# Routed experts of an AdaLN + MoE kernel: rows turned two slots ahead, down product one slot later, three expert homes

## The reference, cut to what matters

```python
# 2048 tokens of width 512 (x: 32 x 64 x 512)
x = x + ffn0(cond0(x))          # layer 0: a 64x64 matrix per batch row, then a dense FFN with LoRA experts
x = x + moe1(cond1(x))          # layer 1:
  # scores = softmax(x @ gate_w); top 2 of 8 experts; H = 352, D = 512
  # g      = silu(x @ w_gate[e]) * (x @ w_up[e])
  # routed = sum over the token's two experts of comb[e] * (g @ w_down[e])
  # shared = silu(x @ sw_gate) * (x @ sw_up) @ sw_down          # hidden width 704
```

## Time and profile before

| | |
|---|---|
| median of 3 runs | 1052.67 us (1052.26 to 1055.33) |
| the profiled execution's own time | 1050.97 us |
| its span, first to last instruction | 1049.1 us |
| busy: PE / PEld / VectorE / ScalarE / GpSimd | 96% / 80% / 50% / 30% / 34% of the span |
| the chain that ended last | PE 85%, DMA 4%, POOL 4%, DVE 2%, issue 1%, ACT 1% |
| mean granted TensorE clock | 0.991 |

### The profile page before, as it was taken

The page is one execution under the profiler, slowest core; times in us unless marked ns, Lnnn a source line. Parts: engine busy times, 40 slices in busy tenths (PEclk is TensorE's granted clock), DMA queues, the critical chain, the costliest instruction groups (busy, mean ns, idle before and its releaser), DMA issues.

```text
span 1049.1 us, 14852 instructions
## 1 busy us (share of the span) xinstructions
PE 1011.8 (96%) x4893; PEld 838.6 (80%) x4895; DVE 525.9 (50%) x886; ACT 314.8 (30%) x550; POOL 354.2 (34%) x351
## 2 busy tenths in 40 slices
PE   7999999999999999999999999999989999999993
PEld 5778887888888888788867777778788999999992
DVE  3797877455574545645666433574543314443100
ACT  2743332111122121211242110301034554545451
POOL 4132344510000000000033000022168989899873
PEclk9999999999999999999999999999999999999997
DMA  6478643534343434444335101004155665565433
GB/s 210 159 252 280 191 132 118 175 130 150 117 131 127 146 127 158 160 155 149 116 145 185 41 1 41 1 1 160 66 178 146 163 161 134 141 144 130 80 60 41
DMA packets 51322, 136.41 MB, mean 130 GB/s; under 512 B 8708, under 2 KB 10004, under 8 KB 50772
## 3 DMA queue, kind: packets, MB, share of 16 engines
q1 hardware_dynamic: 37268, 109.22, 30.4%
q0 software_dynamic: 12432, 25.71, 12.3%
q10 hardware_dynamic: 1584, 1.02, 0.3%
HBM read 96.85 MB, written 39.07 MB: 130 GB/s over the span
## 4 chain that ended last, share of the span: by engine, by line
PE 85%; DMA 4%; POOL 4%; DVE 2%; issue 1%; ACT 1%; SPq 1%; PEldq 0%; POOLq 0%; PEld 0%; DVEq 0%; ACTq 0%
PE ps_y L1677 6%; PE ps_y L1679 6%; PE ps_y L1678 6%; PE ps_h L1637 6%; PE ps_h L1636 6%; PE ps_h L1635 5%; PE ps_u L1690 3%; PE ps_u L1689 3%; DMA out_x<-yt,slot_tok 3%; PE ps_h L1923 2%; PE ps_y L1846 2%; PE ps_y L1847 2%; PE ps_h L1830 2%; PE ps_y L1923 2%; PE ps_y L1918 2%; PE ps_h L1831 2%
## 5 line engine op out<-in xcount | busy, mean ns | idle before, releaser
L1194 DVE TENSOR_TENSOR h<-h,wb 128x512 f32<-128x512 f32 x64 | 44.4, 694 | 162.6 <-ACT h L900 161.2
L894 ACT ACTIVATE h<-ps_h,bias 128x512 f32<-128x512 f32 x64 | 44.0, 689 | 235.1 <-PE ps_h L1644 235.1
L685 POOL DMA_DIRECT2D s_raw<-in_sgu x8 | 4.3, 544 | 299.9 <-DVE g_lo L1202 192.1
L1677 PE MATMUL ps_y<-w_hi,g_hi 128*128 (+1 forms) x256 | 102.6, 401 | 2.3 <-DVE g_lo L1202 2.3
L1679 PE MATMUL ps_y<-w_hi,g_lo 128*128 (+1 forms) x256 | 101.6, 397 | 0.0
L1678 PE MATMUL ps_y<-w_lo,g_hi 128*128 (+1 forms) x256 | 101.5, 396 | 0.0
L1635 PE MATMUL ps_h<-xt_hi,w_hl 128*128 128x512 f32 x256 | 100.1, 391 | 0.7 <-ACT lg_t L843 0.7
L1637 PE MATMUL ps_h<-xt_hi,w_hl 128*128 128x512 f32 x256 | 100.4, 392 | 0.0
L1636 PE MATMUL ps_h<-xt_lo,w_hl 128*128 128x512 f32 x256 | 100.2, 391 | 0.0
L1469 DVE CAST eg_hi<-e_raw 128x704 fp32r<-128x704 f32 x32 | 16.7, 581 | 135.4 <-PE ps_y L1948 122.7
L900 ACT ACTIVATE h<-ps_h,bias 128x512 f32<-128x512 f32 x64 | 43.9, 688 | 114.3 <-PE ps_h L1657 114.3
(11 more groups left out here) (319 smaller groups left out, 2459.8 us busy)
## 6 DMA issues: line engine op xcount, KB each, us to landing
w_hl<-w1s_d SPq DMA_DIRECT2D x49, 704.0 KB, 4.1
w1s_d<-w_hl SPq DMA_DIRECT2D x16, 704.0 KB, 5.9
e_raw<-in_wgu SPq DMA_DIRECT2D x8, 1408.0 KB, 7.2
w_raw<-in_w1b SPq DMA_DIRECT2D x16, 608.0 KB, 4.7
x_in<-in_x SPq DMA_DIRECT2D x4, 1024.0 KB, 5.9
xres<-in_x SPq DMA_DIRECT2D x16, 256.0 KB, 4.6
acc<-x_d SPq DMA_DIRECT2D x4, 1024.0 KB, 7.3
xc_d<-xc SPq DMA_DIRECT2D x4, 1024.0 KB, 4.8
```

Of the source, the lines that this page charges most:

```text
L1194: tt(h1[u][:], h1[u][:], wb[:, v, :], ALU.mult).then_inc(gch, 1)
L1677: mm(ps_y[:, j, :], g_hi[u][:, cols], sl(w2_hi), start=first, **kw)
```

## The change

- TensorE's slot becomes gate(t+1), up(t+1), turn_x(t+3), turn_g(t), down(t-1). GpSimd's becomes products(t+1), x_low(t+3), g_low(t), gather(t+5), scatter_add(t-1). ScalarE's becomes silu(t+1), up(t+1), x_high(t+3), g_high(t), weigh(t-1).
- `xg_hi`, `xg_lo`, `rgt_hi` and `rgt_lo` get two buffers each; `xg` has two instead of four.
- Split weights have three homes, numbers 0, 2, 3 of one tensor `expert`; expert e waits for the last down product of expert e-3. A second table, `home_tab`, packs the homes of six slots, `etab` packs six expert numbers; TensorE reads both at each loop head. VectorE computes `home_tab` at the end of `count_tokens`.
- Before the first slot, gathers 2 to 4 are issued between the first `x_low` steps instead of after them, and three row tiles are turned instead of two.
- The loops run over slots 5 to 32.

```diff
-    WINDOW = 5
+    WINDOW = 6
+    HOMES = (0, 2, 3)
...
-                if t >= 4:
-                    pool.wait_ge(xgt_done, t - 3)
+                if t >= 2:
+                    pool.wait_ge(xgt_done, t - 1)
...
             x_low(0)
+            gather(2)
+            x_low(1)
+            gather(3)
             products(0)
-            x_low(1)
+            x_low(2)
+            gather(4)
             pool.wait_ge(sy_done, NS * TPS)
-            for t in range(2, 5):
-                gather(t)
             for t in range(SLOT_TILES):
-                g_low(t)
                 if t + 1 < SLOT_TILES:
                     products(t + 1)
-                if t + 2 < SLOT_TILES:
-                    x_low(t + 2)
+                if t + 3 < SLOT_TILES:
+                    x_low(t + 3)
+                g_low(t)
                 if t + 5 < SLOT_TILES:
                     gather(t + 5)
                 if t:
                     scatter_add(t - 1)
...
                 if nxt:
                     silu(t + 1, 1 - u)
-                g_high(t, first=stored is None and n == 0)
-                if nxt:
-                    up(t + 1, 1 - u)
-                if nxt2:
-                    x_high(t + 2)
-                weigh(t, n, stored)
+                    up(t + 1, 1 - u)
+                if nxt3:
+                    x_high(t + 3, 1 - u)
+                if nxt:
+                    g_high(t, u, first=isinstance(t, int) and t == 0)
+                if not isinstance(t, int) or t:
+                    weigh(t - 1, (n - 1) % 4, stored)
+                if not nxt:
+                    g_high(t, u)
...
                 nc.vector.tensor_copy(etab[:], etab_g[:]).then_inc(etab_ok, 1)
+
+                dve.wait_ge(etab_ok, 1)
+                for turn in (6.0, 3.0):
+                    link(nc.vector.tensor_scalar(etab_g[:], etab_f[:], turn, -3.0, ALU.is_ge, ALU.mult))
+                    link(tt(etab_f[:], etab_f[:], etab_g[:], ALU.add))
+                link(nc.vector.tensor_scalar(etab_g[:], etab_f[:], 1.0, None, ALU.is_ge))
+                link(tt(etab_f[:], etab_f[:], etab_g[:], ALU.add))
+                link(nc.vector.memset(etab_g[:], 0.0))
+                link(nc.vector.tensor_copy(etab_g[:, 0:windows], etab_f[:, WINDOW - 1:ETAB]))
+                for n in reversed(range(WINDOW - 1)):
+                    link(nc.vector.scalar_tensor_tensor(out=etab_g[:, 0:windows], in0=etab_g[:, 0:windows],
+                                                        scalar=4.0, in1=etab_f[:, n:n + windows],
+                                                        op0=ALU.mult, op1=ALU.add))
+                nc.vector.tensor_copy(home_tab[:], etab_g[:]).then_inc(etab_ok, 1)
...
-                if e >= 2:
-                    tiles = dve.value_load(last_tile[0:1, e:e + 1], min_val=0, max_val=SLOT_TILES)
+                if e >= 3:
+                    tiles = dve.value_load(last_tile[0:1, e - 1:e], min_val=0, max_val=SLOT_TILES)
                     dve.wait_ge(ry_done, 1 + tiles)
...
-                packed = pe.value_load(etab[0:1, bass.ds(t, 1)], min_val=0, max_val=E ** WINDOW - 1)
-                return [(packed // E ** n % E, packed // E ** n % 2) for n in range(WINDOW)]
+                names = pe.value_load(etab[0:1, bass.ds(t, 1)], min_val=0, max_val=E ** WINDOW - 1)
+                places = pe.value_load(home_tab[0:1, bass.ds(t, 1)], min_val=0, max_val=4 ** WINDOW - 1)
+                return [(names // E ** n % E, places // 4 ** n % 4) for n in range(WINDOW)]
...
-                if nxt:
-                    gate_or_up(t + 1, 1 - u, after, 0)
-                turn_g(t)
-                if nxt:
-                    gate_or_up(t + 1, 1 - u, after, 1)
-                if nxt2:
-                    turn_x(t + 2, x_buf, n)
-                down_routed(t, u, this)
+                gate_or_up(t + 1, 1 - u, after, 0)
+                gate_or_up(t + 1, 1 - u, after, 1)
+                if nxt3:
+                    turn_x(t + 3, 1 - u, n)
+                turn_g(t)
+                if behind is not None:
+                    down_routed(t - 1, 1 - u, behind)
...
             gate_or_up(0, 0, e[0], 0)
+            turn_x(1, 1, 16)
             gate_or_up(0, 0, e[0], 1)
-            turn_x(1, 1, 16)
+            turn_x(2, 0, 32)
```

More of the change, by code:

```diff
@@ L214, in adaln_ffn @@
         sb = tensors(routed)
-        eg_hi = sb("eg_hi", [P, 2, DC, 2 * H1], F32R)
-        eg_lo = sb("eg_lo", [P, 2, DC, 2 * H1], F32R)
-        xg = [sb(f"xg{u}", [P, D]) for u in range(2)]
-        e_raw = sb("e_raw", [P, DC * 2 * H1 + HC * D])
-        ed_hi = sb("ed_hi", [P, 2, HC, D], F32R)
-        ed_lo = sb("ed_lo", [P, 2, HC, D], F32R)
-        xg_hi = sb("xg_hi", [P, DC, P], F32R)
-        xg_lo = sb("xg_lo", [P, DC, P], F32R)
+        GU, DN = DC * 2 * H1, HC * D
+        EW = 2 * (GU + DN)
+        homes = ExitStack()
+        expert = tensors(homes)("expert", [P, HOMES[-1] + 1, EW], F32R)
+        homes.close()
+        sb("kept_for_home_0", [P, EW])
+        xg_hi = [sb("xg_hi0", [P, DC, P], F32R)]
+        xg_lo = [sb("xg_lo0", [P, DC, P], F32R)]
         xg_f = sb("xg_f", [P, DC * P])
@@ L226, in adaln_ffn @@
         rg = sb("rg", [P, HC * P])
-        xg += [sb(f"xg{u}", [P, D]) for u in range(2, 4)]
-        rgt_hi = sb("rgt_hi", [P, HC, P], F32R)
-        rgt_lo = sb("rgt_lo", [P, HC, P], F32R)
+        xg = [sb(f"xg{u}", [P, D]) for u in range(2)]
+        e_raw = sb("e_raw", [P, GU + DN])
         rgt_f = sb("rgt_f", [P, HC * P])
+        sb("kept_for_homes_2_3", [P, 3 * EW - (3 * DC * P + 2 * H1 + HC * P + 2 * D + GU + DN + HC * P)])
+        xg_hi += [sb("xg_hi1", [P, DC, P], F32R)]
+        xg_lo += [sb("xg_lo1", [P, DC, P], F32R)]
+        rgt_hi = [sb(f"rgt_hi{u}", [P, HC, P], F32R) for u in range(2)]
+        rgt_lo = [sb(f"rgt_lo{u}", [P, HC, P], F32R) for u in range(2)]
         yt = [sb(f"yt{u}", [P, D]) for u in range(4)]
@@ L341, in adaln_ffn @@
         e_done = sem("e_done")
-        xg_in = [sem(f"xg_in{u}") for u in range(4)]
+        xg_in = [sem(f"xg_in{u}") for u in range(2)]
         xgt_done = sem("xgt_done")
@@ L1922, in gate_or_up @@
                 for c in range(DC):
-                    last = mm(o, xg_lo[:, c, :], w(eg_hi, c), start=False, stop=(c == DC - 1))
+                    last = mm(o, xg_lo[u][:, c, :], w(0, c), start=False, stop=(c == DC - 1))
                 last.then_inc((rgate_done, rup_done)[k], 1)
@@ L1938, in down_routed, with w @@
                     pe.wait_ge(ry_cp, t - 1)
-                w = lambda half, c, k: half[0:k, bass.ds(b, 1), c, :].rearrange("p a n -> p (a n)")
+                def w(low, c, k):
+                    at = 2 * GU + low * DN + c * D
+                    return expert[0:k, bass.ds(b, 1), at:at + D].rearrange("p a n -> p (a n)")
                 o = ps_y[:, 2 + u, :]
```

119 lines of the change are left out of this document (69 added, 50 removed).

## The result

The changed kernel takes **1066.53 us** (median of 4 runs, 1066.08 to 1066.88) against 1052.85 us for the kernel before on the same chip: ratio 1.0129, 95% interval 1.011 to 1.0149. It is slower by about 13.7 us, where 6.1 us less had been forecast. One execution of a later kernel (the register delay with the hold) took 2783 us against 1051 to 1056 for its other eleven; nothing on record explains it, and it is left out of the ratio.

What follows compares the result with a forecast made beforehand. TensorE, busy 96% of the span, was taken as the bound, with GpSimd second to watch. Terms +3.3, +1.65, +3.1, -10.6, +1.3 and -4.85 sum to -6.1, put on the median 1052.67: 1046.6 us, range 1042.8 to 1055.

Steps and rivals of the forecast that it cites:

- term 4: Routed slots: 6.61 us each without waits, -10.6 us; 1.0 us of early waits and 0.3 for loop heads, +1.3.
- term 3: Start of the routed stage: turn_x(2) waits 2.2 us for gather(2); +3.1 us up to the end of down(0).
- Term 1 and 2: Shared stage: the second table's steps add 3.3 us; the longer TensorE wait drops its clock, adding 1.65 us.
- The spare times of 4.8, 5.4 and 9.3 us: Routed slots: slack for g_low, slack for the next slot's products, and time for a gather to land, covering GpSimd's lag.
- The third home frees no wait of TensorE.: Routed slots: a third weight home gains TensorE nothing, as no profile row shows it waiting for weights.
- Term 5: Tail: add 36 goes 1.25 us after down(36), no longer held by slot 38's products; -4.85 us.
- B: Rival, routed slots and tail: GpSimd's single file sets the pace, slots and tail gain nothing; +8.1, 1060.8 us; chance 0.10.
- D: Rival, loop heads: their doubled reads come to light, 5.4 us instead of 0.3; 1051.7 us; chance 0.12.

Runs made afterwards that it cites:

- the register delay with the hold: Changed kernel with homes worked out in registers, a register load before each later expert load, first load held until the third gather landed: 1055.06 us (1.0011).
- the delayed kernel: Changed kernel with homes worked out in registers instead of a second table, plus one register load on SyncE before each later expert load: 1053.76 us (0.9994).

## Why the prediction was wrong, step by step

In the profiled executions the change cost 16.0 us instead of giving 6.1. Of these 22.1 us, term 4 missed 16.9 and term 3 missed 5.4; the others held to 0.3 us.

*Term 1 and 2, right.* 5.07 measured, 4.95 forecast: a step row of 3.1 us and a fall of the clock. The fall lasted two stretches (697.5 to 704.5), of which TensorE worked through little more than one. The Trainium skill's rule ("TensorE: Matmul & The Clock Gate", "What's actually happening"), by which the array falls to half its clock after an idle spell, spoke for it, and the trace agrees: 0.52 and 0.51 behind a wait of 4.8 us.

*Term 3, mis-sized: +8.5, not +3.1.* The issue time was right. The landing was taken over as 5.15 us "with the same load of expert 1 beside it"; but in the earlier trace rows the gather was issued 7.7 us behind that load, and now 1.9 us. It took 8.0, close to the worst end of the range given (8.2). The longer wait brought the clock down again, a second time that no term had: 1.7 us in gate(1), 0.4 in the transposes. The run that held the load shows the cause: 4.0 us for the same gather.

*Term 4, the step that failed.* Mis-sized by 0.09 a slot, 3.1 us: "a slot without waits costs 6.69 - 0.08 = 6.61" took the cheaper up product without the dearer transposes behind it. Then "I take 1.0 us of TensorE waits there ... and 0.3 for the loop heads" became 15.1. The spare times of 4.8, 5.4 and 9.3 us were worked out per operation, from GpSimd's turn without a stall. They were not there even before a stall: the gather said to go out "at about 7.8" went out 11.1 us into its slot (827.61 against 816.51), and was left 6.5 us of the 9.3. One late add (wait 3.5 to 4.0 us) on top of turns that a split has stretched uses them up, and it came at every load, not "now and then", because load and turn had locked in step. Of the 15.1 us, 7.5 are idleness at six loop heads, 1.6 the slot at 0.80 of the clock, and the rest late rows and results. Then the heads: "the sequencer's lead, which hides a head, grows when no wait of TensorE is late" was right as a condition (quiet heads after 957.99 cost 0 to 0.1) and failed where the slot ahead was late, at up to 1.8 us each. The bounds given for the two together, 0 to 15.5, did hold 15.1.

*"The third home frees no wait of TensorE."* True, and the wrong question. It freed VectorE's waits (122.7 us on TensorE before), and with them the place of every load, for one 0.3 us nearer to an add.

*Term 5, right:* -5.1 against -4.85.

*The rivals.* The prediction's B named the right engine and a near sum (1060.8), by another mechanism: GpSimd's work fits (240.3 us without the loads' bytes), its stalls do not. D was half of the loop's loss (7.5 us against 0.3 forecast), but only where a stall came first: without stalls the same heads cost nothing.

What the measurements do not settle is how much of a long slot is the late add, how much the split that has stretched GpSimd's turn and how much the head behind it: the same wait of an add cost TensorE 2.6 to 3.1 us with the others around it (829.91, 859.58, 889.30, 948.67) and 0 to 0.3 in the delayed kernel. Nor do they settle why the load reaches back to an add issued up to 1.1 us ahead of it. In the profile the add of 822.34 lands at 831.3, just behind the load's first part (823.44 + 7.42 = 830.86). The Trainium skill, "DMA: Bandwidth & Descriptors", "Queues, rings and completion order", says that a transfer's semaphore write lands only after every earlier write of the same DMA engine, across its queues; this would make such an add end with the load. The trace fits it here, but no run separates it from plain sharing of the engines.

## What to carry to other kernels

A buffer that takes a wait away also moves what follows it to another place in the cycle than the wait had given it: before adding one, ask which large transfer was timed by that wait, and what it will stand beside when it runs free. Read a transfer's landing time by its distance to the nearest large transfer, not as a median of the stage. Where an in-order list waits for each predecessor's landing, compare the worst landing with the period: at 9 us against 6.7 it stalls by the difference and more (3.5 to 4.0 us here). And when an experiment shifts one transfer away from a load, look at what it shifts towards it.

## What the runs showed that was not expected

- A 2.1 MB expert load makes an add issued up to 1.1 us ahead of it, beside it, or 4.2 us behind it land in 7.6 to 10.3 us instead of 4.8, with an edge of 0.3 us (1.1 to 1.4 us of lead: 9.0 to 5.8).
- VectorE's splits took 18 to 19 us instead of 11 where GpSimd's three element-wise steps followed one another without a pause; two conversions of 128 x 512 that took 1.85 us before (838.97) took 5.00 (816.15).
- A store of 128 bytes ahead of a load on the same queue: the load landed in 9.0 to 12.0 us instead of 7.4 to 8.1.
